# Layer-0 projections of a graph network made trip by trip inside the edge-ranking loop, and layer-1 features normalised in place

## What is computed

```python
def transformer_conv(x, edge_index, wq, bq, wk, bk, wv, bv, ws, bs, heads, out_ch):
    q = (x @ wq + bq).reshape(n, heads, out_ch)
    k = (x @ wk + bk).reshape(n, heads, out_ch)
    v = (x @ wv + bv).reshape(n, heads, out_ch)
    alpha = jnp.sum(q[dst] * k[src], axis=-1) / math.sqrt(out_ch)
    alpha = ...                     # softmax over the edges of each dst
    out = jax.ops.segment_sum(v[src] * alpha[..., None], dst, num_segments=n)
    return out.reshape(n, heads * out_ch) + x @ ws + bs

h = transformer_conv(x, edge_index, w1q, ..., 4, 64)      # layer 0
h = leaky_relu(batch_norm(h, g1, be1))
h = transformer_conv(h, edge_index, w2q, ..., 4, 64)      # layer 1
h = leaky_relu(batch_norm(h, g2, be2))
x = _layernorm(x + h)
# then three relational layers: messages relu(x[src] * (edge_attr @ nn_w.T + nn_b)),
# a mean for each of 3 relations at dst, matrices W[r] and root; a last layernorm
```

## Time and profile before

| | us |
|---|---|
| median of 3 timed runs | 5550.44 |
| lowest and highest | 5524.05, 5554.39 |
| the profiled execution, its time | 5517.37 |
| its span (first to last instruction) | 5515.4 |

### The profile page before, as it was taken

The page is one execution under the profiler, slowest core; times in us unless marked ns, Lnnn a source line. Parts: engine busy times, 40 slices in busy tenths (PEclk is TensorE's granted clock), DMA queues, the critical chain, the costliest instruction groups (busy, mean ns, idle before and its releaser), DMA issues.

```text
span 5515.4 us, 112099 instructions
## 1 busy us (share of the span) xinstructions
PE 3656.3 (66%) x28157; PEld 2826.0 (51%) x28157; DVE 2863.5 (52%) x10477; ACT 1524.4 (28%) x3922; POOL 2690.3 (49%) x2862
## 2 busy tenths in 40 slices
PE   2222266666666866666656777787778778777778
PEld 1111124444444344444435666676666666666667
DVE  5444444445444644444464555554555554555556
ACT  1000002555555155555532222211222221222220
POOL 5556512555555155555545555534555543555550
PEclk6555577898988978998878888898888888888889
DMA  2111125666667156666643222212222321322220
GB/s 45 20 21 22 21 93 175 172 173 170 173 170 167 64 164 174 174 173 169 170 108 103 83 84 83 83 53 79 83 82 84 85 65 59 85 83 80 83 85 30
DMA packets 375434, 563.79 MB, mean 102 GB/s; under 512 B 133582, under 2 KB 261631, under 8 KB 375361
## 3 DMA queue, kind: packets, MB, share of 16 engines
q0 software_dynamic: 155264, 442.19, 29.6%
q1 hardware_dynamic: 165304, 113.92, 7.2%
q10 hardware_dynamic: 54794, 6.81, 0.8%
HBM read 521.54 MB, written 41.08 MB: 102 GB/s over the span
## 4 chain that ended last, share of the span: by engine, by line
PE 32%; issue 18%; DVE 17%; another core or an unknown queue 16%; DVEq 6%; SPq 5%; DMA 4%; ACT 2%; ACTq 0%; POOL 0%; POOLq 0%
PE bank L1074 9%; PE bank L1087 7%; PE bank L963 5%; SPq L782 3%; PE bank L1030 2%; DVE ht L1643 2%; PE bank L1040 2%; DVE region L1723 2%; DVE ht L1630 2%; DMA rings<-edge_attr_T 1%; PE bank L1013 1%; DVEq L650 1%; DVE region L1653 1%; DVE rings L1710 1%
## 5 line engine op out<-in xcount | busy, mean ns | idle before, releaser
L555 POOL DMA_INDIRECT gring<-h_rows,gidx x1248 | 1185.1, 950 | 1031.7 <-DVE rings L1704 682.5
L1074 PE MATMUL bank<-nnwt,rings 128*128 128x256 f32 x3084 | 980.4, 446 | 297.8 <-DMA rings<-edge_attr_T 223.8
L1087 PEld LDWEIGHTS bank<-rings 128*128 128x128 f32 x6168 | 931.4, 221 | 416.1 <-DVE region L1723 264.0
L1087 PE MATMUL bank<-rings 128*128 128x96 f32 x6168 | 952.8, 306 | 272.9 <-DVE region L1723 195.4
L1704 DVE TENSOR_TENSOR rings<-bank,gring 128x256 f32<-128x256 f32 x1542 | 582.1, 419 | 944.1 <-remote 442.2
L1154 ACT ACTIVATE rings<-rings 128x512 f32<-128x512 f32 x771 | 485.6, 630 | 1810.4 <-DVE rings L1704 1348.3
L1074 PEld LDWEIGHTS bank<-nnwt,rings 128*128 128x128 f32 x3084 | 616.4, 222 | 390.7 <-DMA rings<-edge_attr_T 210.3
L1030 PE MATMUL bank<-rings 128*64 128x128 f32 x4096 | 396.4, 322 | 529.2 <-ACT rings L1187 198.5
L523 POOL DMA_INDIRECT gring<-kv_rows,gidx x512 | 489.9, 957 | 467.6 <-PE bank L1056 184.1
L523 POOL DMA_INDIRECT ht<-kv_rows,gidx x512 | 494.7, 966 | 415.4 <-PE bank L1056 238.4
L1723 DVE TENSOR_TENSOR region<-region,bank 128x192 f32 x1542 | 539.1, 350 | 133.2 <-issue 18.8
(11 more groups left out here) (247 smaller groups left out, 4269.7 us busy)
## 6 DMA issues: line engine op xcount, KB each, us to landing
rings<-node_in_window_T SPq DMA_DIRECT2D x256, 128.0 KB
rings<-edge_attr_T SPq DMA_DIRECT2D x1548, 16.0 KB
gring<-h_rows,gidx POOLq DMA_INDIRECT x1248
kv_rows<-rows SPq DMA_DIRECT2D x50, 258.0 KB, 2.6
gring<-kv_rows,gidx POOLq DMA_INDIRECT x512
ht<-kv_rows,gidx POOLq DMA_INDIRECT x512
region<-edge_records SPq DMA_DIRECT2D x13, 576.0 KB, 6.8
edge_records<-rings POOLq DMA_INDIRECT x416
```

The costliest lines, as they stand in the source:

```text
L555: g.indirect_dma_start(out=gring_r[:, 2 * u + k, :], out_offset=None, in_=h_d[l], in_offset=bass.IndirectOffsetOnAxis(ap=gidx_r[:, half, 2 ...
L1074: ins = pe.matmul(bank[slot % RL][:, k * D:(k + 1) * D], eat[:, b, 2 * (slot % 2) + k, :], nnwt[:, :], start=True, stop=True)
L1087: ins = pe.matmul(b[:, (2 * k + c) * SEG:(2 * k + c + 1) * SEG], prod[:, slot % RL, (2 * k + c) * P:(2 * k + c + 1) * P], one, start=True, ...
```

## The change

1. **Layer 0 in the rank loop.** The loops of PE and DVE over the 26 trips are written out instead of being a hardware loop. After the four rank slots of a trip, PE transposes one block of x (`turn_block`, bank 5, trips 0 to 24), makes keys and values of the block before (`keys_of_block`, bank 6, trips 1 to 25) and one 512-column product of q or s (`queries_of`, bank 7, trips 4 to 25). DVE empties them at the end of its part of the trip (`keep_keys`, `keep_queries`). So 22 of the 28 products of q and s are made there (`QSLOOP`) and 6 are left for `project` (two of 512 columns and four of 128).
2. **DVE's order within a trip.** Instead of all one-hots and then all rows, DVE now does the rows of a slot and right after them the one-hot of the same slot of the next trip.
3. **SP.** The loads of x and the stores of keys and values go with the trips; the store of the job tables (`tab`) and its wait come behind them, and DVE no longer waits for that store. The tables move from `ht` to spare room in `gring` and `rings`.
4. **Layer 1 in place.** After attention 0, ACT normalises `st` onto itself and DVE's leaky ReLU works on `st`; the layer-1 products read `st`. `ht` is free then, and POOL's wait for the projections goes.
5. **Skip products of layer 1 later.** The 14 s products of layer 1 are made after attention 1, two for each group of four transposed blocks, and ACT, not DVE, adds their bias and writes them to `st`.

```diff
+NB4 = 512 // P
+QSLOOP = min(GTRIPS - NB4, 4 * (NP // 512))
@@ gather_layer (POOL)
-                    elif seq == 1 and u == U // 2:
-                        g.wait_ge(s_proj, sum(NPROJ))
@@ sync_program
             sp.wait_ge(event("rows_cleared"), 1)
-            sp.wait_ge(event("tab"), 1)
-            sp.dma_start(tab_d, tab).then_inc(s_tab, 16)
-            for i in range(NT):
-                load_rows(i, s_proj, i - 1 if 2 <= i < NT - 1 else None)
+            for i in range(2):
+                load_rows(i, None, None)
             for l in range(2):
-                kv_base = NT if l == 0 else NPROJ[0]
                 for i in range(NT):
-                    sp.wait_ge(s_pev, kv_base + i + 1)
+                    if l == 0 and i + 2 < NT:
+                        load_rows(i + 2, s_proj, turned_job(i) if i + 2 < NT - 1 else None)
+                    sp.wait_ge(s_pev, NPROJ[0] + i + 1 if l else kv_job(i))
                     sp.dma_start(kv_d[l][i * P:(i + 1) * P, :], kvrow[:, i % 2, :]).then_inc(s_kvo[i % 2], 16)
                 if l == 0:
+                    sp.wait_ge(event("tab"), 1)
+                    sp.dma_start(tab_d, tab).then_inc(s_tab, 16)
@@ tensor_program, ranks
-            for slot in range(GU):
-                ranks(0, slot)
-            with pe.Fori(1, GTRIPS - 1) as trip:
+            for trip in range(GTRIPS):
                 for slot in range(GU):
                     ranks(trip, slot)
-            for slot in range(GU):
-                ranks(GTRIPS - 1, slot)
+                if trip < NT:
+                    turn_block(pe, trip)
+                if 1 <= trip <= NT:
+                    keys_of_block(pe, 0, trip - 1, bank[6])
+                if NB4 <= trip < NB4 + QSLOOP:
+                    queries_of(pe, 0, *qs_of(trip - NB4), bank[7])
             pe.wait_ge(s_row, ROWSTEPS * G)
+            pe.wait_ge(s_pev, jobs_before(GTRIPS))
@@ tensor_program, after the attention of a layer
+                if l:
+                    pe.wait_ge(s_kt, 2 * PAIRS)
+                    pe.wait_ge(s_acc, 2 * T)
                 for j in range(NT):
+                    if l and j % NB4 == 0:
+                        nb = j // NB4
+                        if nb >= 2:
+                            pe.wait_ge(s_skip, 2 * (nb - 1))
+                        for c in range(2):
+                            queries_of(pe, l, 3, c, nb, bank[2 + 2 * (nb % 2) + c])
                     pe.wait_ge(event("divided"), l * NT // DG + j // DG + 1)
@@ new helpers (PE)
+        def turn_block(pe, i):
+            slot = 2 if i == NT - 1 else i % 2
+            pe.wait_ge(s_xr[slot], 16 * (1 if slot == 2 else i // 2 + 1))
+            if i:
+                pe.wait_ge(s_pev, turned_job(i - 1))
+            for c in range(2):
+                ins = pe.transpose(bank[5][:, c * P:(c + 1) * P], xr[:, slot, c * P:(c + 1) * P], ident[:, :])
+            ins.then_inc(s_proj, 1)
+        def queries_of(pe, l, k, c, nb, b):
+            n = min(512, NP - nb * 512)
+            if l == 0:
+                pe.wait_ge(s_pev, turned_job(min(NT, (nb + 1) * NB4) - 1))
+                j = 4 * nb + 2 * (k // 3) + c
+                if 0 < j < QSLOOP:
+                    pe.wait_ge(s_pev, qs_job(j - 1))
+            for kc in range(2):
+                ins = pe.matmul(b[:, 0:n], wts[:, l, k, kc, c * P:(c + 1) * P],
+                                (st if l else ht)[:, kc, nb * 512:nb * 512 + n], start=kc == 0, stop=kc == 1)
+            ins.then_inc(s_proj, 1)
@@ scalar_program
+                if l:
+                    for nb in range(NB):
+                        n = min(512, NP - nb * 512)
+                        act.wait_ge(s_proj, sum(NPROJ) + 2 * nb + 2)
+                        for c in range(2):
+                            act.activation(st[:, c, nb * 512:nb * 512 + n], bank[2 + 2 * (nb % 2) + c][:, 0:n], ACT.Identity,
+                                           bias=bias_s[:, l, c:c + 1]).then_inc(s_skip, 1)
-                act.wait_ge(s_proj, sum(NPROJ[:l + 1]))
-                        ins = act.activation(ht[:, c, block], st[:, c, block], ACT.Identity, bias=bn_t[:, c, 3:4],
+                        ins = act.activation((ht if l else st)[:, c, block], st[:, c, block], ACT.Identity, bias=bn_t[:, c, 3:4],
@@ vector_program, ranks
-            for slot in range(GU):
-                rows_of(0, slot)
-            with v.Fori(1, GTRIPS) as trip:
-                for slot in range(GU):
-                    one_hot(trip, slot)
+            for trip in range(GTRIPS):
                 for slot in range(GU):
                     rows_of(trip, slot)
+                    if trip + 1 < GTRIPS:
+                        one_hot(trip + 1, slot)
+                if trip < NT:
+                    v.wait_ge(s_proj, turned_job(trip))
+                    v.tensor_copy(ht[:, :, trip * P:(trip + 1) * P], bank[5][:, 0:2 * P].rearrange("p (c n) -> p c n", c=2))\
+                        .then_inc(s_pev, 1)
+                if 1 <= trip <= NT:
+                    ...
+                    keep_keys(v, 0, trip - 1, kv_job(trip - 1), bank[6])
+                if NB4 <= trip < NB4 + QSLOOP:
+                    ...
+                    keep_queries(v, 0, *qs_of(trip - NB4), qs_job(trip - NB4), bank[7])
@@ vector_program, adding the sums
                     v.wait_ge(s_tr, l * NT + j + 1)
+                    if l and j % NB4 == 0:
+                        v.wait_ge(s_skip, 2 * (j // NB4) + 2)
@@ tables_of_tiles
-            v.wait_ge(s_tab, 16)
```

More of the change, by code:

```diff
@@ L408, in build @@
         s_pev = sem("s_pev")
+        s_skip = sem("s_skip")
         s_kvo = [sem(f"s_kvo{i}") for i in range(2)]
@@ L983, in free @@
+        def project(pe, l):
+            if l == 0:
+                for j in range(QSLOOP, 4 * NB):
+                    if j >= QSLOOP + 4:
+                        pe.wait_ge(s_pev, qs_job(j - 4))
+                    queries_of(pe, 0, *qs_of(j), bank[j % 4])
+                return
+            job = NPROJ[0]
             def free(job):
[L984 to L985 removed]
+                pe.wait_ge(s_pev, job - 3)
                 return bank[job % 4]
[L988 to L997 removed]
@@ L1606, in projected @@
-                    ins.then_inc(s_pev, 1)
-                    job += 1
-            v.wait_ge(s_vec, vec_n.n)
-            for c in range(2):
-                for nb in range(NB):
-                    n = min(512, NP - nb * 512)
-                    v.wait_ge(s_proj, job + 1)
-                    v.tensor_scalar(st[:, c, nb * 512:nb * 512 + n], bank[job % 4][:, 0:n], bias_s[:, l, c:c + 1], None, ALU.add)\
-                        .then_inc(s_pev, 1)
+                    keep_queries(v, l, 0, c, nb, job + 1, bank[job % 4])
```

156 lines of the change are left out of this document (83 added, 73 removed).

## The result

The changed kernel takes 5376.79 us (median of 4, 5355.44 to 5385.41) where the kernel before takes 5548.68 us (median of 4, 5524.05 to 5554.39): ratio 0.9693, 95% interval 0.9652 to 0.9733, 172 us. The profiled execution took 5355.4 us against 5517.4, 162 us less. The forecast was 119 us less.

What follows compares the result with a forecast made beforehand. The rank stage was taken as bound by a circle of POOL's bursts and held PE increments, not work. Terms -115 + 0 - 20 + 16 = -119 us, from 5537, gave 5418, say 5420 us; 8-in-10 range 5300 to 5500.

Steps and rivals of the forecast that it cites:

- The projection stage, -115: Between rank tables and unpacking of records: six jobs left, unpacking starts at 730 instead of 847.5 us, net -115 us.
- The rank circle, 0: Rank trips: new work fits under POOL's scatter burst with 3 us slack, trip stays 26.8 us, so 0 us.
- by the row of the first slot: Rank stage: the first slot gets through during POOL's burst, 4.9 us after PE started it; grounds for taking 0.
- the circle gets shorter: Rival, rank stage: more slots pass per burst; five instead of four save 34 us, all pauses closed 160; chance 0.23.
- the code is longer. 0 to +20: Rank loops of PE and DVE written out 25 times: fetching could show, 0 to +20 us; no chance of its own.
- The new work: Rank trips: added PE and DVE work hides; rival that it lands in POOL's pause, +25 to +90 us, chance 0.22.
- signs of being wrong: Rank stage: long DVE waits before emptyings, two POOL pauses per trip, trips well off 26.8 us, scatters over 0.97 us.
- The rule of the Trainium skill on VectorE's two-port mode: Rank trips: emptyings would block GpSimd's descriptor writes, lengthening bursts by up to 2.8 us each, 70 us; chance 0.02.
- Layer 1, start, -20: Start of attention 1: it waits for q alone, not the last s bank; between -19 and -25, taken as -20 us.
- Layer 1, end, +16: Behind attention 1: groups with two skip products take 6.6 against 3.6 us, +16 us; bounds 0 to 21.5.
- ACT empties within PE's time: Behind attention 1: ACT's emptying of the skip products adds nothing to a group's 6.6 us.
- only the first pair hides: Behind attention 1: only the first pair of skip products is covered, behind reciprocal and division, from 2823.5 us.

Runs made afterwards that it cites:

- The skip edit: Changed kernel with layer 1's skip products issued one group of four blocks ahead, on three pairs of banks instead of two: 0.9960 to the kernel before, free chip.
- before_interleaved: Kernel before with VectorE making the next trip's one-hots of a slot right behind that slot's rows, loops kept: 0.9979, free chip.
- after_again: The changed kernel, unchanged, run again on a free chip: 0.9978 to the kernel before.
- before_again: The kernel before, unchanged, run again on a free chip for a profile: 4238.05 us.

## Why the prediction was right, and where not

*The projection stage, -115.* Right: -117.8. The first unpacking came at 680.6 us, which is 730 less the 49 us of the ranks.

*The rank circle, 0.* Here is the error: the term was -49 us, and the profiled execution beat the sum of -119 by 43 us (the other stretches together missed by 6 us the other way). I took 0 "by the row of the first slot", with one hold on one slot per trip, and expected one pause of about 6.5 us in each trip. The first rival, "the circle gets shorter", came about, and in its own way: a burst now takes in six slots on average, not five, so there are 16 pauses instead of 25, and 49 us go where five slots had given 34. The time fell inside the stated range because the range had left room for this rival, not because the term was right. Why more slots get through is not shown. The rival's reason was that one-hots come slot by slot; the order was tried only on free chips.

The runs also show a gain from what I had set aside as "the code is longer. 0 to +20": with straight code on TensorE and VectorE, in the old order and without the projections, the scatters end 32 us earlier and the first unpacking comes 25 us earlier. But there the trips keep one pause each and the pauses get cheaper, while in the changed kernel there are fewer and they cost as much as before. So the 49 us are not shown to be a sum of 32 for the straight code and 17.5 for the rest. In a loop trip TensorE's sequencer has ten instructions of registers and branches beside the 48 products, and VectorE's has 39; in straight code there are four semaphore waits on each. Instructions pass slowly in a burst, so fewer should mean an earlier increment. That step is argued: the run took the loop out of both engines at once, and the one with nine products for twelve met only free chips. The Trainium skill, "Runtime: NRT & Kernel Launch", section "Instruction fetch mechanics", says that straight code is fetched ahead while a taken branch can stall. Both runs of the straight kernel agree in sign (0.9974 and 0.9967); neither shows a fetch. Whether the order or the projections' products make the bursts longer stays open.

*The new work.* Right in that it hid in the trips, PE 311 us busy instead of 173, and no second pause per trip appeared. One of the signs of being wrong did appear: long waits at the emptyings, seven of up to 5.7 us in front of L1659 (31.2 us). They were not for PE, as I had feared, but for VectorE's own increments, whose delay the prediction had no term for. What these waits cost is not separated; the stage got shorter in spite of them. The rule of the Trainium skill on VectorE's two-port mode ("SBUF — State Buffer", section "SBUF: two separate sides"), which the prediction gave a chance of 0.02, shows no price here: the scatters' median stayed 970 ns, and 25 scatters took over 1.1 us where it was 10 before, 3.5 us more in all. No run shows whether an emptying is such an operation.

*Layer 1, start, -20.* Right: -18.0. The first score product came 26 us after SP's last store (1719.9).

*Layer 1, end, +16.* Right in kind, mis-sized: +24.6. The step "ACT empties within PE's time" failed: a group is a chain of products (3.6 us), ScalarE's copies (1.4) and the part of VectorE's additions that the last transposes wait for (2.3), 7.35 us and not 6.6. The step "only the first pair hides" failed in part: that pair ran at half clock, 5.39 us, and the first addition came 2.8 us later than in before. One more group at half clock cost 1.7 us. The skip edit takes ScalarE's link out of the chain and gives back 7.8 us.

*The level.* The prediction held for the kind of chip that it was argued from. It had no case for the other kind, where the same reasoning (the projections are open because the ranks end with the scatters) turns the largest term into nothing.

*A version that beats both.* The changed kernel with the skip products a group ahead: 0.9960 to before on a free chip where the changed kernel has 0.9978. On a holding chip it was not tried; its edit touches only the stretch behind attention 1, which is alike on both.

## What to carry to other kernels

Before removing a stage from behind a loop, ask what makes that loop end so late: the 115 us were worth 118 where the ranks were held to the pace of the scatters, and nothing where they ran 200 us ahead. Where engines are slowed while another issues indirect DMAs, writing a loop out can pay: it was worth 19 us here (0.9967), though which engine's loop control it was is not shown. Count the pauses and their cost apart; two edits with nearly the same end of the stage worked in different ways. When a product is moved to the end of a stage, count the engine that empties it as a link of the chain, and issue it one group ahead.

## What the runs showed of the hardware

TensorE, and VectorE too, can be held while GpSimd issues a stream of indirect DMAs, on some chips and not on others. On holding chips single products start 1.5 to 2.8 us apart in a burst and TensorE's increments arrive up to 14 us late. In the changed kernel VectorE's own increments reach VectorE up to 5.7 us late, in both holding traces of it (44 and 30 waits of over 1 us in the ranks); the three traces with the old order show no such wait. On free chips the ranks' increments arrive after 0.01 us in the same burst, and no trace has a wait of VectorE for itself of over 1 us in the ranks. The two kinds differ by far more than the ranks: the same kernel takes 4238 or 5549 us, attention 0 691 or 917 us. The free chip's kernel before, attention 0 and the relational layers:

```profile
648.00:1339.00 691.00, 508.44 (x7776) 360.92 (x7772) 461.42 (x2513) 444.13 (x1406) 493.61 (x506) 0.96 0.79 217
2187.00:4236.00 2049.00, 1757.01 (x10552) 1475.47 (x10552) 1406.45 (x3873) 504.42 (x822) 1247.07 (x1375) 0.99 0.34 98
```

DVE and POOL do the same work in the same busy time as in the changed kernel's relational layers on the holding chip, where PE's granted clock was 0.85 instead of 0.99:

```profile
2737.00:5353.00 2616.00, 2032.95 (x10549) 1751.19 (x10547) 1406.57 (x3873) 504.44 (x822) 1238.52 (x1372) 0.85 0.26 76
```

What makes a chip hold its engines is not shown by any run here, nor how much of the difference outside the ranks is the hold. The mean granted clock of a run is 0.80 to 0.83 on holding chips and 0.91 to 0.94 on free ones, but that alone does not give the time: one run of the kernel before on a free chip had 0.83 and took 4273.59 us.

A second, smaller thing: on free chips the scatters of the kernel before come 1.315 us apart and those of before_interleaved and after_again 1.286 to 1.287 us, 11 to 12 us over 415 steps, more than the gain of either on such a chip (8.8 and 5.4 us). In before_again 27 scatters took over 1.1 us, and 25 of them overlapped VectorE's running totals (L1299) and the steps around it; 78 others overlapped L1299 too and were not long. The 27 account for 7.5 us, against 1.8 us for 7 such scatters in after_again, so for about half of the 12. Why the order changes this was not tried.
